# Expert rows left over from whole units: 22 tiles of 128 rows, or 8 tiles and 11 pairs of 64-row chunks

## The chip, the cores and the metric

The kernel runs on one core of one Trainium2 chip. The metric is the device time of one execution in microseconds. Three executions of the kernel before took 1140.57, 1143.54 and 1146.61 us (median 1143.54).

## The reference

One transformer layer on `x` of 4 x 1024 tokens of 256 float32 values: a Nystrom attention, then a mixture of 8 experts of which each token takes 2. Only the experts are touched by the change.

```python
x = x + attention(layernorm(x))        # 16 heads, 64 landmarks, pseudo-inverse, convolution of 13 taps
h_in = layernorm(x)                    # 4096 tokens of 256
logits = h_in @ router_w.T             # 8 experts
weights, selected = sparsemixer(logits) # two experts per token, one weight each
for e in range(8):
    h = silu(h_in @ w_gate[e].T) * (h_in @ w_up[e].T)      # 256 -> 512
    out += dense_w[:, e:e+1] * (h @ w_down[e].T)           # 512 -> 256
x = x + out
```

## The kernel before

The program is written out by hand, engine by engine, with semaphores; nothing reorders it. TensorE multiplies, ScalarE (`act`) applies functions and copies, VectorE (`dve`) does the elementwise work, GpSimd (`pool`) scatters rows by index, SyncE (`sp`) issues the plain transfers.

The router gives 8192 rows (4096 tokens, 2 experts each). GpSimd scatters each into the region of its expert in the scratch tensor `xs_d`; a row carries its 256 values, its weight and its token number. Then the rows are worked off in **items**. An item belongs to one expert and is a list entry in `ITEMS` with its number of 128-row blocks:

- 3 early items (5 blocks) of the fullest expert, while the router still works;
- 22 **units** of two blocks (`NU`), which are full but for the last rows of an expert;
- 22 **tiles** of one block (`NT`), for what is left of each expert. With 8 experts and ends that don't divide by 128 some rows of tiles are padding.

That is 71 blocks. VectorE works out which expert and which first row each unit and tile has, once the router's counts are there: `table` writes `u_eid`, `u_row` for units, and after `units_taken` the same for tiles.

Work goes in steps `n`, one step per block: a unit has two (its 512 inner columns in two halves), a tile one. In a step:

- TensorE `hidden(0, n)`: the gate product. Stationary is a 128x128 piece of the weights `wgu`, moving are the item's rows as columns (`xst`, 256 columns for a unit, 128 for a tile), two contractions of 128. The result has the inner dimension on partitions. Each float32 matmul stands in the trace as two passes.
- TensorE `x_columns(a+1)`: the next item's rows transposed into bank 7. `rows_transposed` on ScalarE copies them to `xst`.
- TensorE `down(n-1)`: stationary is the hidden block `hid` of the step before, moving are the down weights `w_d_s[:, e]` (256 columns), addressed by the expert's number in a register. Results go to bank 4 or 6.
- TensorE `hidden(1, n)`: the up product, like the gate.
- ScalarE `gate_out(n)`: the Silu of the gate. VectorE `hidden_out(n)`: times the up product, into `hid`.
- VectorE `rows_weighed(a-1)`: the down result times the row weights into one of 8 buffers `ys` (`YRING`). `expert_weights(a+2)` copies an expert's gate and up weights (128x2048) into one of two `wgu` buffers.
- GpSimd `add_rows`: an indirect transfer that adds the 128 rows to `out` by token number. Before an item's first store it waits until all stores of the item before have landed, since a token's two rows may lie in two items of different experts.
- SyncE `unit_rows`, `tile_rows`: an item's rows from `xs_d` into one of 16 slots `xs`.

The last item's stores end the kernel.

Of the kernel before, what the change touches and what calls it, by code (L numbers as in the profile page):

```python
# [27 lines left out]
P = 128  # L28
# [74 lines left out]
FIRST = NEARLY  # L103
CHOSEN = [i + 4 for i in DONE[:LATE]] + [QT + 1, QT + 2, QT + 4]
# [17 lines left out]
def down_bank(a, b):  # L122
    return 4 + 2 * (b if ITEMS[a] == 2 else a % 2)

# [43 lines left out]
def layer(nc, x, w_qkv, wq_t, wk_t, conv_band, w_fc, b_fc, router_t, w_gu, w_down, out):  # L168
    with ExitStack() as ctx:
# [112 lines left out]
        hid = ex[:, 0].rearrange("p (u c) -> p u c", u=2)  # L282

# [27 lines left out]
        assert NT <= NU  # L311
        t_tau, u_eid, u_row, t_eid, t_row = (sb(f"tab{i}", NU) for i in range(5))
        early = sb("early", 2)
        n_pad = sb("n_pad", E)
        tokid = sb("tokid", G * 2).rearrange("p (v c) -> p v c", v=G)
# [32 lines left out]
        def _(sp):  # L348
# [79 lines left out]
            def slot_free(a):  # L428
                for r in range(BLOCK[a] - XRING, BLOCK[a + 1] - XRING):
                    if r >= EBLK:  # L430
                        sp.wait_ge(s(f"m_sc{r % YRING}"), 16 * (r // YRING + 1))

            def unit_rows(i):
                a = FIRST + i
                v = (BLOCK[a] - EBLK) % XRING
                slot_free(a)
                r = sp.value_load(u_row[0:1, i:i + 1].bitcast(I32), min_val=0, max_val=ZROW - 2 * P)
                sp.dma_start(xs[:, v:v + 2], xs_d[bass.ds(r, 2 * P), :].rearrange("(u p) c -> p u c", p=P))\
                  .then_inc(s(f"m_rows_in{i % 8}"), 16)

            def tile_rows(i):
                a = FIRST + NU + i
                slot_free(a)
                sp.wait_ge(s("m_xtp"), a - 7)
                r = sp.value_load(t_row[0:1, i:i + 1].bitcast(I32), min_val=0, max_val=ZROW)
                sp.dma_start(xs[:, (BLOCK[a] - EBLK) % XRING], xs_d[bass.ds(r, P), :])\
                  .then_inc(s(f"m_rows_in{(NU + i) % 8}"), 16)

            for i in range(4):
                unit_rows(i)  # L450
            for e in range(E):
                pad_region(sp, e)
            for i in range(4, NU):
                unit_rows(i)
            sp.wait_ge(s("d_tiles"), 1)
# [1395 lines left out]
```

## Time and profile before

| | |
|---|---|
| median of the three executions | 1143.54 us |
| the profiled execution | 1153.58 us |
| its span | 1151.8 us |
| TensorE busy | 1100.0 us, 96% |
| VectorE, ScalarE, GpSimd busy | 632.0, 303.1, 300.5 us |
| mean granted clock of TensorE | 0.987 |
| units and tiles, from the first unit's gate product to the last down product | 783.4 to 1143.6 us |

The profile is one execution, a little slower than the three without profile. The span runs from the first to the last instruction. Busy shares are averages over stages; the stage of units and tiles is the last third. A row of the chain of waits is a piece of work that the next one waited for; in a timeline, the bracket behind a row is how long the engine was idle before it and what ended that.

### The profile page before, as it was taken

Reading aid. Unit: us, or ns where it says so; the run is one execution under the profiler, and the core shown is the slowest. Engines: PE = TensorE matmul, PEld = TensorE weight load, DVE = VectorE, ACT = ScalarE, POOL = GpSimd, SP = SyncE. Lnnn points to the kernel's source line nnn. Section 1 sums busy time; section 2 is a strip of 40 time slices with the busy share of each in tenths; the row PEclk is TensorE's granted clock in tenths of the full one; section 3 lists DMA queues with packets and bytes.
Section 4 is the critical chain, followed back from the end, with each engine's and each line's share of the span. In section 5 each row is a group of like instructions: output and inputs, shape, how many; then the busy total and the mean of one; then the engine's idle time right before and its main releaser. Section 6 shows DMA issues by size and latency. Waiting matters only on the chain.

```text
span 1151.8 us, 22825 instructions
## 1 busy us (share of the span) xinstructions
PE 1100.0 (96%) x9162; PEld 915.3 (79%) x9162; DVE 632.0 (55%) x1346; ACT 303.1 (26%) x457; POOL 300.5 (26%) x298
## 2 busy tenths in 40 slices
PE   4999999999989899999999999879999999999996
PEld 4887888888888656777776777767888888899996
DVE  7466666555478565586677677653233233234442
ACT  4433323332234421333233233221111111111110
POOL 6000000000200022244543563532322322334343
PEclk9999999999999999999999999889999999999998
DMA  9200000001200131222222233334323323221221
GB/s 340 107 1 1 1 1 1 1 1 38 57 3 1 52 134 37 102 74 86 101 83 75 76 103 122 111 87 101 48 49 52 47 49 52 34 46 35 45 27 11
DMA packets 48538, 68.91 MB, mean 60 GB/s; under 512 B 7872, under 2 KB 41792, under 8 KB 47424
## 3 DMA queue, kind: packets, MB, share of 16 engines
q1 hardware_dynamic: 34720, 47.50, 12.9%
q0 software_dynamic: 13296, 16.92, 8.8%
q10 hardware_dynamic: 432, 3.24, 0.7%
q8 instruction: 62, 1.02, 0.4%
q14 instruction: 28, 0.23, 0.1%
HBM read 42.10 MB, written 26.46 MB: 60 GB/s over the span
## 4 chain that ended last, share of the span: by engine, by line
PE 86%; DVE 7%; issue 2%; POOL 2%; ACT 1%; another core or an unknown queue 1%; POOLq 0%; DVEq 0%
PE ps L1737 20%; PE ps L1760 10%; PE ps L1624 10%; PE ps L1663 9%; PE ps L1375 9%; PE ps L1336 9%; PE ps L1655 5%; PE ps L1643 1%; PE ps L1490 1%; PE ps L1310 1%; PE ps L1720 1%; PE ps L1509 1%; ACT mem L691 1%; PE ps L1390 1%
## 5 line engine op out<-in xcount | busy, mean ns | idle before, releaser
L1737 PE MATMUL ps<-mem 128*128 128x256 f32 (+1 forms) x1504 | 259.9, 328 | 0.0
L1737 PEld LDWEIGHTS ps<-mem 128*128 128x128 f32 x1504 | 232.3, 191 | 21.2
L565 POOL DMA_INDIRECT out<-mem x71 | 122.9, 1731 | 255.8 <-DVE mem L1215 192.5
L1207 DVE TENSOR_TENSOR mem<-mem,ps 128x512 f32<-128x512 f32 x71 | 48.8, 687 | 171.6 <-PE ps L1737 143.1
L1760 PE MATMUL ps<-mem 128*128 x568 | 137.2, 385 | 5.1 <-DVE mem L1207 3.4
L535 POOL TENSOR_TENSOR mem<-mem,small 128x1024 f32<-128x1024 f32 x36 | 68.6, 1906 | 242.1 <-DVE small L1144 109.3
L1624 PE MATMUL ps<-mem 128*128 128x512 f32 x288 | 129.7, 594 | 1.3 <-DVE mem L1028 1.3
L771 ACT ACTIVATE mem<-ps 128x512 f32<-128x512 f32 x71 | 42.4, 597 | 320.9 <-PE ps L1737 314.7
L1760 PEld LDWEIGHTS ps<-mem 128*128 128x128 f32 x568 | 105.8, 193 | 18.4 <-issue 5.7
L1663 PE MATMUL ps<-mem 128*128 128x256 f32 x512 | 120.1, 388 | 0.0
L1375 PE MATMUL ps<-mem 128*128 128x256 f32 x512 | 119.2, 386 | 0.6 <-ACT mem L645 0.6
L1336 PE MATMUL ps<-mem 128*128 128x256 f32 x512 | 114.5, 380 | 0.0
L1663 PEld LDWEIGHTS ps<-mem 128*128 128x128 f32 x512 | 95.9, 192 | 14.1 <-issue 2.1
L1375 PEld LDWEIGHTS ps<-mem 128*128 128x128 f32 x512 | 95.9, 192 | 13.9 <-issue 0.8
L1336 PEld LDWEIGHTS ps<-mem 128*128 128x128 f32 x512 | 95.6, 190 | 12.7 <-issue 0.3
L1624 PEld LDWEIGHTS ps<-mem 128*128 128x128 f32 x288 | 54.2, 190 | 56.2 <-issue 52.7
L549 POOL DMA_INDIRECT xs_d<-mem,idx x64 | 62.5, 976 | 58.0 <-DVE idx L1124 37.9
L1655 PEld LDWEIGHTS ps<-mem 128*64 128x64 f32 x1152 | 58.0, 138 | 22.1 <-issue 22.1
L1215 DVE TENSOR_SCALAR mem<-ps,mem 128x256 f32<-128x256 f32 x71 | 32.1, 480 | 72.8 <-PE ps L1760 72.8
L1655 PE MATMUL ps<-mem 128*64 128x116 f32 x1152 | 66.1, 268 | 3.0 <-POOL mem L535 3.0
L746 ACT ACTIVATE mem<-ps 128x928 f32<-128x928 f32 (+2 forms) x36 | 31.5, 875 | 109.8 <-PE ps L1655 102.2
L1224 DVE COPY mem<-mem 128x2048 f32 x44 | 54.1, 1229 | 4.2 <-issue 0.9
(219 smaller groups left out, 1302.5 us busy)
## 6 DMA issues: line engine op xcount, KB each, us to landing
mem<-w_gu SPq DMA_DIRECT2D x9, 1024.0 KB, 5.1
mem<-xs_d SPq DMA_DIRECT2D x22, 260.0 KB, 2.8
mem<-x SPq DMA_DIRECT2D x8, 512.0 KB, 7.5
mem<-x SPq DMA_DIRECT2D x32, 128.0 KB, 2.2
out<-mem SPq DMA_DIRECT2D x32, 128.0 KB, 1.7
mem<-w_down SPq DMA_DIRECT2D x8, 512.0 KB, 5.8
xnt_d<-mem ACTq DMA_DIRECT2D x3, 1056.0 KB, 5.0
mem<-xnt_d SPq DMA_DIRECT2D x3, 1056.0 KB, 4.9
```

Of the source, the lines that this page charges most:

```text
L535: pool.tensor_tensor(a1[:, u], ex[:, u].rearrange("p (h c) -> p h c", h=H), ri[:, 16 * u:16 * u + 16].unsqueeze(2).to_broadcast([P, H, M]) ...
L549: pool.indirect_dma_start(out=xs_d, out_offset=bass.IndirectOffsetOnAxis(ap=idx[:, u, v, c:c + 1].bitcast(U32), axis=0), in_=xd[:, u, v, c ...
L565: pool.indirect_dma_start(out=out_rows, out_offset=bass.IndirectOffsetOnAxis(ap=rows[:, D + 1:D + 2].bitcast(U32), axis=0), in_=ys[:, r % ...
L1207: dve.tensor_tensor(hid[:, n % 2], sil[:, n % 2], bank(2 + n % 2), ALU.mult).then_inc(s("m_hid"), 1)
L1224: dve.tensor_copy(wgu[:, w % 2], w_gu_s[:, e]).then_inc(s("m_w"), 1)
L1336: mm = pe.matmul(bank(t // 2)[:, t % 2 * 2 * P:(t % 2 + 1) * 2 * P], xnts[b][:, k, HALO + P * t:HALO + P * t + P], g3c[:, b, k, j * P:(j + ...
L1375: mm = pe.matmul(bank(6)[:, k * 2 * P:(k + 1) * 2 * P], xna[:, b, t, k * P:(k + 1) * P], e3s[m % 4][:, t], start=(t == 0), stop=(t == RT - 1))
L1624: mm = pe.matmul(bank(2 * u + half), xnt2[b % 2][:, k, TO * t:TO * t + P], g1c[:, b, k, 512 * half:512 * half + 512], start=(k == 0), stop ...
L1655: mm = pe.matmul(bank(4, 2)[c:c + 64, (h // 2) * P:(h // 2) * P + TO], a1[:, q % 2, h], band[:, h], start=True, stop=True)
L1663: mm = pe.matmul(bank(6)[:, 0:D], cvt[:, j, at_:at_ + P], pm[:, b, j], start=(j == 0), stop=(j == J - 1))
L1737: mm = pe.matmul(bank(2 * c + n % 2)[:, i * size:(i + 1) * size], w[:, k, c, f * P:(f + 1) * P], xst[:, a % 2, k, 0:size], start=(k == 0), ...
L1760: mm = pe.matmul(bank(down_bank(a, b))[:, 0:D], hid[:, u, i * size + b * P:i * size + (b + 1) * P], w_d_s[:, e, f], start=(f == 0), stop=( ...
```

## The change

The padding of the tiles is cut by a smaller grain. Of an expert's rows, whole units are taken first, then whole tiles of 128 rows (8, `NT`), and what remains in **chunks** of 64 rows. Two chunks, mostly of two different experts, make a **pair** (11, `NP`): one block of 128 rows. The blocks are 68. Units and tiles keep their code; the order of items is 3 early, five rounds of 4 units and 2 pairs, 1 pair, 7 tiles, 2 units, 1 tile (`KIND`). A pair differs so:

- its two chunks come by two transfers, and the rows' token numbers are split in `half_to`, so that each of two stores writes one chunk; the second store waits for the landing of the first;
- hidden products: the rows are stationary, 64 columns a chunk, and the weights move, 512 columns; the first chunk works in columns 0 to 63 of the array, with its expert's weights taken by register from `w_gu_s`, the second in 64 to 127 with the copy in `wgu`. The result has rows on partitions;
- `inner_transposed`: `hid` is transposed in four pieces into bank 5, `inner_columns` on ScalarE copies them to `hidt`;
- `down`: stationary are 64 columns of `hidt` a chunk, moving the down weights of the first expert by register and of the second from `w_d_c`, a copy that `second_down_weights` on ScalarE makes; there is one such buffer. `down` of a pair stands behind `hidden(1)` of the next step, not ahead of it;
- VectorE makes one more table (`c_eid`, `c_row`, 22 chunks), in the second step of the first unit.

```diff
-NT = (LATER + E * (P - 1)) // P - 2 * NU
+NT = -(-(LATER - E * (P - 1)) // P) - 2 * NU
+C = P // 2
+NC = (LATER + E * (C - 1)) // C - 2 * (2 * NU + NT)
+NP = -(-NC // 2)
 EBLK = EROWS // P
-ITEMS = [2] * (EBLK // 2) + [1] * (EBLK % 2) + [2] * NU + [1] * NT
 NEARLY = EBLK // 2 + EBLK % 2
+ROUNDS = min(NU // 4, NP // 2)
+KIND = ["early"] * NEARLY + (["unit"] * 4 + ["pair"] * 2) * ROUNDS + ["pair"] * (NP - 2 * ROUNDS) + \
+       ["tile"] * (NT - 1) + ["unit"] * (NU - 4 * ROUNDS) + ["tile"]
+ITEMS = [2] * (EBLK // 2) + [1] * (EBLK % 2) + [2 if kind == "unit" else 1 for kind in KIND[NEARLY:]]
+ORDER = [KIND[:a].count(kind) for a, kind in enumerate(KIND)]
...
+def stores(r):
+
+    return sum(2 if KIND[STEP_OF[n][0]] == "pair" else 1 for n in range(r % YRING, r + 1, YRING))
+
+
+def loads(a):
+
+    return sum(2 if KIND[i] == "pair" else 1 for i in range(FIRST + (a - FIRST) % 8, a + 1, 8))
...
+        hidt = ex[:, 1, 0:F].rearrange("p (f c) -> p f c", f=4)
+        w_d_c = at(7 * SQ + 2 * G * 2 * ROW, 4 * D).rearrange("p (f c) -> p f c", f=4)
...
+            def item_rows(a):
+                i, v, landed = ORDER[a], (BLOCK[a] - EBLK) % XRING, s(f"m_rows_in{(a - FIRST) % 8}")
+                if KIND[a] == "unit":
+                    r = sp.value_load(u_row[0:1, i:i + 1].bitcast(I32), min_val=0, max_val=ZROW - 2 * P)
+                    sp.dma_start(xs[:, v:v + 2], xs_d[bass.ds(r, 2 * P), :].rearrange("(u p) c -> p u c", p=P)).then_inc(landed, 16)
+                if KIND[a] == "tile":
+                    if i == 0:
+                        sp.wait_ge(s("d_tiles"), 1)
+                    r = sp.value_load(t_row[0:1, i:i + 1].bitcast(I32), min_val=0, max_val=ZROW)
+                    sp.dma_start(xs[:, v], xs_d[bass.ds(r, P), :]).then_inc(landed, 16)
+                if KIND[a] == "pair":
+                    if i == 0:
+                        sp.wait_ge(s("d_chunks"), 1)
+                        sp.wait_ge(s("d_pad_out"), 16 * (E + 1))
+                    for q in range(2):
+                        r = sp.value_load(c_row[0:1, 2 * i + q:2 * i + q + 1].bitcast(I32), min_val=0, max_val=ZROW)
+                        sp.dma_start(xs[C * q:C * q + C, v], xs_d[bass.ds(r, C), :]).then_inc(landed, 16)
+
+            for a in range(FIRST, FIRST + 4):
+                item_rows(a)
...
+            ch.link(pool.memset(half_out[:, :], 2.0 * TOK))
+            for q in range(2):
+                ch.link(pool.affine_select(out=half_out[:, q:q + 1], in_=half_out[:, q:q + 1], compare_op=ALU.is_ge, fill=0.0,
+                                           base=(-C, C - 1)[q], pattern=[[0, 1]], channel_multiplier=(1, -1)[q]))
...
+                    rows = xs[:, (r - EBLK) % XRING]
+                    if KIND[a] == "pair":
+                        add_rows(r, half_to[:, ORDER[a] % 4, 0:1])
+                        wait_alone(pool, f"m_sc{r % YRING}", 16 * stores(r) - 16)
+                        add_rows(r, half_to[:, ORDER[a] % 4, 1:2])
+                    else:
+                        add_rows(r, rows[:, D + 1:D + 2])
 
...
+            def second_down_weights(a):
+                if ORDER[a] == 0:
+                    act.wait_ge(s("d_chunks"), 1)
+                e = act.value_load(c_eid[0:1, 2 * ORDER[a] + 1:2 * ORDER[a] + 2].bitcast(I32), min_val=0, max_val=E - 1)
+                if ORDER[a] >= 1:
+                    act.wait_ge(s("m_down"), BLOCK[max(b for b in range(a) if KIND[b] == "pair") + 1])
+                act.activation(w_d_c, w_d_s[:, e], ACT.Copy).then_inc(s("m_wdc"), 1)
+
+            def inner_columns(n):
+                a = STEP_OF[n][0]
+                act.wait_ge(s("m_ht"), ORDER[a] + 1)
+                if ORDER[a] >= 1:
+                    act.wait_ge(s("m_down"), BLOCK[max(b for b in range(a) if KIND[b] == "pair") + 1])
+                act.activation(hidt, bank(5).rearrange("p (f c) -> p f c", f=4), ACT.Copy).then_inc(s("m_hidt"), 1)
...
+                if KIND[STEP_OF[n - 1][0]] == "pair":
+                    inner_columns(n - 1)
+                if KIND[a] == "pair":
+                    second_down_weights(a)
                 if h == ITEMS[a] - 1 and a + 1 < len(ITEMS):
                     rows_transposed(a + 1)
...
+                    if KIND[a] == "pair":
+                        ch.link(dve.tensor_tensor(half_to[:, ORDER[a] % 4].bitcast(I32),
+                                                  rows[:, D + 1:D + 2].bitcast(I32).to_broadcast([P, 2]),
+                                                  half_out[:, :].bitcast(I32), ALU.add))
...
-            units_taken()
-            table(P, P - 1, 7, NT, t_eid, t_row, "d_tiles")
+            taken(NU, 2 * P)
+            table(P, 0, 7, NT, t_eid, t_row, "d_tiles")
             expert_weights(FIRST + 1)
             rows_weighed(1)
             hidden_out(4)
             dve.wait_ge(s("d_tiles"), 1)
             for n in range(BLOCK[FIRST], NSTEP):
                 a, h = STEP_OF[n]
-                if h == 0:
+                if h == 0 and KIND[a - 1] != "pair":
                     rows_weighed(a - 1)
                 hidden_out(n)
+                if h == 0 and KIND[a - 1] == "pair":
+                    rows_weighed(a - 1)
+                if n == BLOCK[FIRST] + 1:
+                    taken(NT, P)
+                    table(C, C - 1, 6, 2 * NP, c_eid, c_row, "d_chunks")
                 if h == ITEMS[a] - 1 and a + 2 < len(ITEMS):
                     expert_weights(a + 2)
...
+                if KIND[a] == "pair":
+                    if c == 0:
+                        if ORDER[a] == 0:
+                            pe.wait_ge(s("d_chunks"), 1)
+                        first_expert[a] = expert_of(c_eid, 2 * ORDER[a])
+                        pe.wait_ge(s("m_w"), a - FIRST + 1)
+                        pe.wait_ge(s("m_xst"), a + 1)
+                        pe.wait_ge(s("m_hid"), n - 1)
+                    for k in range(KD):
+                        for q in range(2):
+                            mm = pe.matmul(bank(2 * c + n % 2)[C * q:C * q + C], xst[:, a % 2, k, C * q:C * q + C],
+                                           (w_gu_s[:, first_expert[a]] if q == 0 else wgu[:, (a - FIRST) % 2])[:, k, c], start=(k == 0), stop=(k == KD - 1))
+                    mm.then_inc(s(("m_gate", "m_up")[c]), 1)
+                    return
...
+            def inner_transposed(n):
+                a = STEP_OF[n][0]
+                pe.wait_ge(s("m_hid"), n + 1)
+                if ORDER[a] >= 1:
+                    pe.wait_ge(s("m_hidt"), ORDER[a])
+                for f in range(4):
+                    mm = pe.transpose(bank(5)[:, f * P:(f + 1) * P], hid[:, n % 2, f * P:(f + 1) * P], idt)
+                mm.then_inc(s("m_ht"), 1)
 
             def down(n):
                 (a, h), u = STEP_OF[n], n % 2
-                e = expert(a)
-                pe.wait_ge(s("m_hid"), n + 1)
+                if KIND[a] != "pair":
+                    e = expert(a)
+                    pe.wait_ge(s("m_hid"), n + 1)
+                else:
+                    pe.wait_ge(s("m_hidt"), ORDER[a] + 1)
+                    pe.wait_ge(s("m_wdc"), ORDER[a] + 1)
                 size = ITEMS[a] * P
                 per = F // size
-                before = a - 2 if ITEMS[a] == 1 and ITEMS[a - 2] == 1 else a - 1
+                before = a - 2 if ITEMS[a] == 1 and a >= 2 and ITEMS[a - 1] == 1 else a - 1
                 if h == 0 and before >= 0:
                     pe.wait_ge(s("m_y"), BLOCK[before + 1])
-                for b in range(ITEMS[a]):
-                    for i in range(per):
-                        f = per * h + i
-                        mm = pe.matmul(bank(down_bank(a, b))[:, 0:D], hid[:, u, i * size + b * P:i * size + (b + 1) * P],
-                                       w_d_s[:, e, f], start=(f == 0), stop=(f == 3))
+                if KIND[a] == "pair":
+                    for f in range(4):
+                        for q in range(2):
+                            mm = pe.matmul(bank(down_bank(a, 0))[C * q:C * q + C, 0:D], hidt[:, f, C * q:C * q + C],
+                                           w_d_s[:, first_expert[a], f] if q == 0 else w_d_c[:, f], start=(f == 0), stop=(f == 3))
+                else:
...
                 hidden(0, n)
+                after_pair = KIND[STEP_OF[n - 1][0]] == "pair"
+                if after_pair:
+                    inner_transposed(n - 1)
                 if h == ITEMS[a] - 1 and a + 1 < len(ITEMS):
                     x_columns(a + 1)
-                if n > first:
+                if n > first and not after_pair:
                     down(n - 1)
                 hidden(1, n)
+                if after_pair:
+                    down(n - 1)
             down(NSTEP - 1)
```

On TensorE, a step of the tiles before (L1737 hidden products, L1720 `x_columns`, L1760 `down`):

```order
L1737 MATMUL ps<-mem 128x128 x8
L1737 MATMUL ps<-mem 128x128 [waits m_hid,m_xst,m_w]
L1737 MATMUL ps<-mem 128x128 x7
L1720 MATMUL ps<-ids,mem 128x128 [waits m_xst,m_rows_in3]
L1720 MATMUL ps<-ids,mem 128x128
L1746 TENSOR_LOAD tab
L1746 ISA x2
L1760 ISA [waits m_y,m_hid]
L1760 MATMUL ps<-mem 128x256
L1760 ISA
```

The second pair's step and the start of the unit behind it, in the changed program (L1804 hidden products of a pair, L1839 `inner_transposed`, L1784 `x_columns`, L1858 `down` of a pair, L1820 hidden products of a unit):

```order
L1804 ISA [waits m_hid,m_xst,m_w]
L1804 MATMUL ps<-mem 64x512 x2
...
L1839 MATMUL ps<-ids,mem 128x128 [waits m_hid]
L1839 MATMUL ps<-ids,mem 128x128 x3
L1784 MATMUL ps<-ids,mem 128x128 [waits m_xst,m_rows_in6]
...
L1804 MATMUL ps<-mem 64x512 x2
L1858 ISA [waits m_y,m_wdc,m_hidt]
L1858 MATMUL ps<-mem 64x256 x2
...
L1820 MATMUL ps<-mem 128x256 [waits m_hid,m_xst,m_w]
L1820 MATMUL ps<-mem 128x256 x3
```

The down products have moved from between the two hidden products of a step to behind both, directly ahead of the next item's gate product; the transposes of the inner rows are new.

On ScalarE, the tiles before (L771 `gate_out`, L764 `rows_transposed`):

```order
L771 ACTIVATE mem<-ps 128x512 [waits m_hid,m_gate]
L764 ACTIVATE mem<-ps 128x2x128 [waits m_up,m_xtp]
L771 ACTIVATE mem<-ps 128x512 [waits m_hid,m_gate]
L764 ACTIVATE mem<-ps 128x2x128 [waits m_up,m_xtp]
L771 ACTIVATE mem<-ps 128x512 [waits m_hid,m_gate]
```

And in the changed program, the second pair's step (L804 `gate_out`, L819 `inner_columns`, L809 and L812 `second_down_weights`, L797 `rows_transposed`):

```order
L804 ACTIVATE mem<-ps 128x512 [waits m_hid,m_gate]
L819 ACTIVATE mem<-ps 128x512 [waits m_down,m_ht]
L809 TENSOR_LOAD tab
L809 ISA x2
L812 ISA [waits m_down]
L812 ACTIVATE mem<-mem 128x1024
L797 ACTIVATE mem<-ps 128x512 [waits m_up,m_xtp]
L804 ACTIVATE mem<-ps 128x512 [waits m_hid,m_gate]
```

Between the gate's Silu and the copy of the next item's columns there are now the copy of the inner columns and the copy of the down weights, which waits for `m_down`.

## Rows read from the trace of the kernel before

**Rows 1.** The page, part 4: the chain that ended last, by engine
```profile
PE 86%; DVE 7%; issue 2%; POOL 2%; ACT 1%; another core or an unknown queue 1%; POOLq 0%; DVEq 0%
```

**Rows 2.** The chain in order of time, units: start us, us, what
```profile
990.81 3.45 PE ps L1737 x16
...
994.26 0.44 PE ps L1720 x4
...
1001.61 3.45 PE ps L1737 x16
```

**Rows 3.** The same view, tiles
```profile
1104.31 1.73 PE ps L1760 x8
...
1109.83 1.73 PE ps L1760 x8
```

**Rows 4.** The same view around one convolution (L1655)
```profile
654.09 1.74 PE ps L1655 x32
...
655.83 3.65 PE ps L1663 x16
...
659.48 3.43 PE ps L1624 x8
```

**Rows 5.** Groups by line and form, ScalarE: busy us, mean ns | idle before
```profile
L752 ACT ACTIVATE mem<-mem 128x1024 f32<-128x1024 f32 x36 | 37.9, 1052 | 18.5 <-DVE mem L1134 18.2
...
L764 ACT ACTIVATE mem<-ps 128x512 f32<-128x512 f32 x24 | 14.2, 592 | 8.3 <-PE ps L1720 8.3
...
L764 ACT ACTIVATE mem<-ps 128x256 f32<-128x256 f32 x23 | 8.7, 378 | 0.0
```

**Rows 6.** Timeline of the end: start us, us, engine, line, what
```profile
1138.97 0.49 DVE L1215 TENSOR_SCALAR mem<-ps,mem 128x256 f32<-128x256 f32 x1 [2.77 <-PE ps L1760]
...
1140.81 0.69 DVE L1207 TENSOR_TENSOR mem<-mem,ps 128x512 f32<-128x512 f32 x1 [1.35 <-PE ps L1737]
...
1141.65 1.99 PE L1760 MATMUL ps<-mem 128*128 x8 [0.94 <-DVE mem L1207]
...
1143.68 0.48 DVE L1215 TENSOR_SCALAR mem<-ps,mem 128x256 f32<-128x256 f32 x1 [2.18 <-PE ps L1760]
...
1145.32 1.56 POOL L565 DMA_INDIRECT out<-mem  x1 [3.46 <-issue]
```

**Rows 7.** Timeline, first unit: VectorE, and one TensorE row
```profile
772.76 0.17 DVE L1197 TENSOR_SCALAR small<-small 128x8 f32<-128x8 f32 x1
...
776.71 0.24 DVE L1192 TENSOR_SCALAR tab<-tab,small 128x22 int32<-128x22 f32 x1
...
777.46 1.23 DVE L1224 COPY mem<-mem 128x2048 f32 x1 [0.51 <-issue]
...
793.06 0.69 DVE L1207 TENSOR_TENSOR mem<-mem,ps 128x512 f32<-128x512 f32 x1 [4.93 <-PE ps L1737]
...
796.46 0.88 DVE L1215 TENSOR_SCALAR mem<-ps,mem 128x256 f32<-128x256 f32 x2 [1.41 <-PE ps L1760]
...
798.24 0.69 DVE L1207 TENSOR_TENSOR mem<-mem,ps 128x512 f32<-128x512 f32 x1 [0.91 <-issue]
...
800.15 1.89 PE L1760 MATMUL ps<-mem 128*128 x8
```

**Rows 8.** The chain in order of time, at the start
```profile
6.33 0.20 POOL validf L489
...
6.59 0.20 POOL validf L491
```

**Rows 9.** Timeline of GpSimd, last unit and first tile
```profile
1027.52 1.56 POOL L565 DMA_INDIRECT out<-mem  x1 [0.31 <-issue]
...
1032.98 1.55 POOL L565 DMA_INDIRECT out<-mem  x1 [3.89 <-issue]
```

**Rows 10.** Timeline of TensorE behind two waits
```profile
768.34 1.99 PE L1760 MATMUL ps<-mem 128*128 x8 [1.69 <-DVE mem L1215]
...
780.22 3.42 PE L1760 MATMUL ps<-mem 128*128 x8 [2.43 <-DVE mem L1207]
```

More of the change, by code:

```diff
@@ L103 @@
 FIRST = NEARLY
+assert all(ITEMS[a] == 1 or (BLOCK[a] - EBLK) % 2 == 0 for a in range(FIRST, len(ITEMS)))
 CHOSEN = [i + 4 for i in DONE[:LATE]] + [QT + 1, QT + 2, QT + 4]
@@ L441, in tile_rows @@
[L441 to L450, printed above, removed]
+                        sp.wait_ge(s(f"m_sc{r % YRING}"), 16 * stores(r))
@@ L451, in _ @@
+            for a in range(FIRST, FIRST + 4):
+                item_rows(a)
             for e in range(E):
                 pad_region(sp, e)
-            for i in range(4, NU):
-                unit_rows(i)
-            sp.wait_ge(s("d_tiles"), 1)
-            sp.wait_ge(s("d_pad_out"), 16 * (E + 1))
-            for i in range(NT):
-                tile_rows(i)
+            for a in range(FIRST + 4, len(ITEMS)):
+                item_rows(a)
             for v in range(YRING):
-                sp.wait_ge(s(f"m_sc{v}"), 16 * -(-(BLOCK[-1] - v) // YRING))
+                sp.wait_ge(s(f"m_sc{v}"), 16 * stores(max(r for r in range(BLOCK[-1]) if r % YRING == v)))
@@ L1031, in _ @@
                 ch.step(dve.tensor_copy(v, v.bitcast(I32)))
+            ch.step(dve.tensor_copy(half_out[:, :].bitcast(I32), half_out[:, :]))
             ch.sync()
@@ L1193, in table, with taken @@
                    .then_inc(s(done), 1)
[L1195 to L1197 removed]
+            def taken(count, rows):
+                ch.link(dve.tensor_scalar(te, te, -1.0, float(count), ALU.mult, ALU.add))
                 ch.link(dve.scalar_tensor_tensor(out=te, in0=te, scalar=0.0, in1=nt, op0=ALU.max, op1=ALU.min))
[L1199 to L1200 removed]
+                ch.step(dve.scalar_tensor_tensor(out=base, in0=te, scalar=float(rows), in1=base, op0=ALU.mult, op1=ALU.add))
+                ch.link(dve.scalar_tensor_tensor(out=n_e, in0=te, scalar=-float(rows), in1=n_e, op0=ALU.mult, op1=ALU.add))
             def hidden_out(n):
@@ L1218, in expert_weights @@
             def expert_weights(a):
-                w, n = a - FIRST, a - FIRST - NU
-                source = u_eid[0:1, w:w + 1] if n < 0 else t_eid[0:1, n:n + 1]
+                w, i = a - FIRST, ORDER[a]
+                source = {"unit": u_eid, "tile": t_eid, "pair": c_eid}[KIND[a]]
+                i = 2 * i + 1 if KIND[a] == "pair" else i
+                source = source[0:1, i:i + 1]
                 e = dve.value_load(source.bitcast(I32), min_val=0, max_val=E - 1)
@@ L1741, in expert @@
             def expert(a):
-                i, t = a - FIRST, a - FIRST - NU
-                if t == 0:
-                    pe.wait_ge(s("d_tiles"), 1)
-                source = early[0:1, 0:1] if i < 0 else u_eid[0:1, i:i + 1] if t < 0 else t_eid[0:1, t:t + 1]
-                return pe.value_load(source.bitcast(I32), min_val=0, max_val=E - 1)
+                if KIND[a] == "early":
+                    return expert_of(early, 0)
+                if KIND[a] == "unit":
+                    return expert_of(u_eid, ORDER[a])
@@ L1755, in down @@
                 if h == 0 and before >= 0:
                     pe.wait_ge(s("m_y"), BLOCK[before + 1])
-                for b in range(ITEMS[a]):
-                    for i in range(per):
-                        f = per * h + i
-                        mm = pe.matmul(bank(down_bank(a, b))[:, 0:D], hid[:, u, i * size + b * P:i * size + (b + 1) * P],
-                                       w_d_s[:, e, f], start=(f == 0), stop=(f == 3))
+                if KIND[a] == "pair":
[4 more added lines that the diff above has]
+                else:
+                    for b in range(ITEMS[a]):
+                        for i in range(per):
+                            f = per * h + i
+                            mm = pe.matmul(bank(down_bank(a, b))[:, 0:D], hid[:, u, i * size + b * P:i * size + (b + 1) * P],
+                                           w_d_s[:, e, f], start=(f == 0), stop=(f == 3))
```

39 lines of the change are left out of this document (18 added, 21 removed).

## The prediction, made before the changed kernel ran

> **What bounds the kernel now.** I read the page's chain of waits first: 86% of the span lies on TensorE [rows 1]. Then the same chain in order of time, over the stage that the change touches, because a share of the span says nothing about one stage. There TensorE's pieces follow each other without a hole: a unit (two blocks of 128 rows) has a period of 1001.61 - 990.81 = 10.80 us, 5.40 a block, with four transposes in 0.44, 0.109 each [rows 2]; a tile (one block) has 1109.83 - 1104.31 = 5.52 us [rows 3]. Nothing else is late in this stage, so a TensorE instruction taken out there is worth its time, and one put in, or a wait, costs its own.
>
> **What the change takes out.** Expert rows before: 5 early blocks, 22 units, 22 tiles, 71 blocks. After: 8 tiles and 11 pairs stand for the 22 tiles, 68 blocks. Fourteen tiles go: 14 x 5.52 = **-77.3 us** [rows 3].
>
> **What a pair costs on TensorE.** The hidden products of a pair are 8 matmuls of 512 columns with 64 stationary columns, each in the trace two passes: 16 passes, 8 in each column half. Eight passes of 512 columns take 3.43 us on the full array [rows 4], so 3.43 if the halves run side by side, 6.86 if not. The convolution is the one large user of column halves before: 32 passes of 116 columns in 1.74 us [rows 4]. At 3.43 / (8 x 512) us a column one after the other they would need 3.1, in two halves 1.55; the halves do overlap there. The down products are 16 passes of 256 columns, two halves: the 1.73 of a tile [rows 3]. New are four transposes of the inner rows, 0.44, and the two of the rows stay, 0.22. A pair: 3.43 + 1.73 + 0.44 + 0.22 = 5.82; eleven: **+64.0 us**. So a pair as such is 0.3 dearer than a tile, and three blocks fewer would leave -13.3.
>
> **Changes between full and half width.** The convolution takes 1.74 where its columns ask for 1.55, and the 16 passes of 256 columns after it take 3.65 [rows 4] where the same kind takes 2 x 1.73: 0.19 + 0.19 = 0.38 for going into halves and coming back. By the order, two pairs between units have four stretches of halves (first half of the hidden products of the first; its second half with the first of the next; the second half of that with down of the first; down of the last) and the three pairs in a row have five: 4 x 4 + 5 = 21. 21 x 0.38 = **+8.0 us**; bounds 21 x 0.19 = 4 and 21 x 0.5 = 10.
>
> **The wait that is added.** `second_down_weights(a)` copies the second expert's down weights on ScalarE (128x1024) into the one buffer `w_d_c`. For the second of two adjoining pairs it waits on `m_down` of the first. But TensorE now does that `down` last in the step, after `hidden(1, n)`, and behind the waiting copy in ScalarE's queue stands `rows_transposed(a+1)`, which TensorE's next instruction, `hidden(0, n+1)`, needs. So TensorE stands still for the whole way: end of matmul to the engine 0.04 and an address instruction 0.06 (an estimate), the copy 1.05 (the nearest row is the exponential of 128x1024 in memory, 1052 ns [rows 5]), the column copy 0.59 for a unit or 0.38 for a single block [rows 5], 0.10 of overlap between two ScalarE instructions (an estimate), 0.15 back to TensorE (1140.81 + 0.69 to 1141.65) [rows 6]: 1.79 or 1.58 us idle. An unstalled follower also overlaps the drain, 1.89 against 1.73, 0.16 [rows 3, 7], and 0.1 of the return from halves is hidden in the wait. Net 1.85 before a unit (four times), 1.74 before the third pair, 1.64 before a tile: **+10.8 us** for six. Bounds: the copy at half its time gives 7.6, a slower hand-over 13. A lone first pair has no such wait: its copy waits on a down that is long over and has `down` and `hidden(1)` of 3.4 us as cover. The inner-row copy to columns (`inner_columns`, 0.6) has the transposes and `hidden(1)`, 2.2 us, as cover and costs nothing; without that cover it would cost 0.6 a pair.
>
> **The chunk table on VectorE.** `taken` and `table` run once more, in the first unit's second step. The same work took from 772.76 to 776.95, 4.2 us, and 0.5 passed until the copy behind it began [rows 7]. Placed after the 0.69 that starts at 793.06, it ends near 797.9; the weight copy (1.23) then runs to 799.7, `rows_weighed` (0.88) to 800.5, and the product that began at 798.24 begins 2.2 later. Before, the product was there at 799.1 with its 0.15 of hand-over and TensorE asked at 800.15 [rows 7]; now it is there at 801.3: **+1.1 us** (0 to 2.2).
>
> **Start and end.** Three short GpSimd instructions are added ahead of `consts`. GpSimd's constants are on the chain from the first microsecond, 0.26 from one such instruction to the next [rows 8]: **+0.7 us** (0.5 to 0.8). At the end the last tile now follows a unit, not a tile. A unit's second store starts 1.56 + 0.31 = 1.87 behind its first; the start after it came 1032.98 - 1027.52 = 5.46 later [rows 9], as it waits for the landing. In the last step the tile's rows come 4.7 behind the unit's (the two VectorE starts at 1138.97 and 1143.68 are as far apart), and their store would start 1.15 after them (1143.68 + 0.48 to 1145.32 [rows 6]), at 5.85; through the unit's stores it starts at 1.15 + 1.87 + 5.46 = 8.5. That is 2.6; I take **+2.2 us** because landings are uneven, bounds 0 and 2.6.
>
> **Nothing for:** GpSimd's two stores per pair, one after the other's landing, some 10.9 us a pair against 8 on TensorE. Eight buffers (`YRING`) lie between, and each unit gives back 10.8 - 7.3 = 3.5. The seven tiles behind the three pairs hold the lag of about 8 us near constant; that is below two blocks. Nothing for SyncE: `item_rows` of the first pair stands behind `d_chunks` (near 798) and is needed four units on, near 821.
>
> **Sum.** -77.3 + 64.0 + 8.0 + 10.8 + 1.1 + 0.7 + 2.2 = **+9.5 us**. The profiled execution took 1153.58, so 1163.1 there; the median of the runs shown is 1143.54, and nothing in the sum depends on the 10 us between them: 1153.0.
>
> **Rivals.**
> 1. *TensorE's clock falls in the new waits.* After 1.69 us idle eight passes still took 1.99; after 2.43 us idle the same took 3.42, half speed, which is the lower level of 1.2 GHz [rows 10]. The new waits of 1.6 to 1.8 lie near the first and short of the second. Each fall costs about 3.42 - 1.73 = 1.7. Two to six falls: +3.4 to +10.2, 1156 to 1163. Chance 0.2.
> 2. *The halves overlap only in part.* For: two 512-column streams side by side are longer than any before. Against: [rows 4]. The other end of the bound is 3.43 + 1.73 = 5.16 more a pair, 11 times: 1210. Overlap wanting a quarter: about +15, 1168. Chance 0.06. The Trainium skill, "TensorE: Matmul & The Clock Gate", Measured speedup vs the span model, gives 2.38 times for three column tiles, 0.79 of the ideal; an estimate by that page is 5.16 / 0.79 - 5.16 = 1.4 more a pair, 1168 in all. This case's trace does not agree so far: 3.1 / 1.74 is 1.8 times of a possible 2, with the change of width included.
> 3. *Not slower: the copy hardly holds TensorE.* If ScalarE's copy in memory is much quicker than the exponential, or the way through the two semaphores shorter, the six waits shrink. At 0.9 us each the sum is +3.9, 1147; with no wait at all it is -1.3, 1142. From under 1.2 us a wait on the case is inside half a per cent. For it: no row shows a plain copy of this shape. Against: two of the three rows of the chain are measured, and the order leaves no other work between [rows 5, 6]. Chance 0.24. Only if the changes of width were free as well would the kernel be faster: -13.3 + 1.1 + 0.7 + 2.2 = -9.3, 1134; that is 0.05 of these 0.24.
>
> **Numbers.** Likeliest is the sum, chance 0.5, own range 1149 to 1158 from the bounds of the waits and of the width changes. The range for 8 in 10 takes in most of rival 1 and the better half of rival 3: 1145 to 1164. A measurement of this kernel tells about half a per cent (5.7 us; the three runs shown spread over 6.0) from no change. Slower by more: 0.75 (the forecast, rivals 1 and 2, less a little); within: 0.20; faster by more: 0.05.
>
> **What would show it.** In the changed profile: passes of 512 columns with 64 stationary columns in couples, about 1.7 us for each half of the hidden products (above 2.0 speaks for rival 2); six idle pieces of TensorE of 1.6 to 1.8 us with ScalarE's column copy as what ended them, and the weight copy before it near 1.05 us; a granted clock that stays at 1.00 behind them (rival 1 if not); two single tiles still at 5.52; one piece of about 1 us near 800 us; the last store starting about 8 us, not 6, after the weighing of the rows before it. I am wrong if the idle pieces are missing, or if TensorE's time for two pairs without them is far from 2 x 5.82 + 4 x 0.38 = 13.2 us.

## The result, and the profile after

| | before | changed |
|---|---|---|
| median (range, runs) | 1143.53 us (1140.57 to 1146.61, 4) | 1152.74 us (1151.76 to 1154.46, 4) |
| profiled execution, its span | 1153.58, 1151.8 | 1151.76, 1149.9 |
| matmul passes of TensorE, its busy time | 9162, 1100.0 us | 8992, 1088.0 us |

The changed kernel is slower: ratio 1.0078, 95% interval [1.006, 1.0096], 9.2 us on the medians. The two profiled executions stand the other way round: that of before took 1153.58 us, while the 51 other executions of it on record took 1140.6 to 1147.2. The chain of waits of before, in order of time (start us, us, what):

```profile
744.44 6.25 another core or an unknown queue
...
750.74 3.63 another core or an unknown queue
```

The view's chain of the changed kernel begins only at 789.64 us, so it can't tell of this place; ScalarE's timeline can. Ahead of the Silu at 750.71 and the activation at 754.38 ScalarE idled 6.28 and 3.07 us before, and no such piece (0 and 0.89 us) ahead of the same two at 741.00 and 742.46 in the changed kernel. So the two are compared by stages that begin after it, or end before it.

**The waits behind the second pair.** The chain of the changed kernel in order of time, second pair of the first round (L1804 hidden products of a pair, L1839 `inner_transposed`, L1784 `x_columns`, L1858 `down` of a pair, L1820 hidden products at full width), with the five later idle pieces:

```profile
824.45 1.87 PE ps L1804 x8
826.32 1.73 PE ps L1858 x16
828.04 1.79 issue
829.83 1.96 PE ps L1820 x8
...
886.00 1.79 issue
...
943.97 1.79 issue
...
1001.92 1.79 issue
...
1059.66 1.68 issue
...
1067.67 1.57 issue
```

Six pieces, 10.41 us together, where [rows 2, 3] have none. "Issue" says that the view found no releaser. The timeline of the same microseconds shows one (start us, us, engine, line, tile and shape, in brackets the idle time before and what ended it):

```profile
826.15 1.90 PE L1858 MATMUL ps<-mem 128*64 x16
...
828.19 1.06 ACT L812 ACTIVATE mem<-mem 128x1024 f32 x1 [3.54 <-PE ps L1858]
...
829.15 0.58 ACT L797 ACTIVATE mem<-ps 128x512 f32<-128x512 f32 x1
...
829.83 0.89 PE L1820 MATMUL ps<-mem 128*128 128x256 f32 x3 [1.79 <-issue]
```

ScalarE idles 3.54 us until TensorE's `down` ends, copies the weights in 1.06, then the columns in 0.58, and 0.10 after those TensorE starts.

**The stages.** At the table of chunks, the chain:

```profile
790.03 0.61 DVE mem L1260
790.64 0.14 issue
790.78 1.99 PE ps L1864 x8
792.77 3.45 PE ps L1820 x16
```

This `down` at 790.78 is the one that stands at 800.15 before [rows 7]. The end, timeline:

```profile
1134.05 0.88 DVE L1272 TENSOR_SCALAR mem<-ps,mem 128x256 f32<-128x256 f32 x2 [2.77 <-PE ps L1864]
1135.48 1.56 POOL L592 DMA_INDIRECT out<-mem  x1 [7.33 <-DVE mem L1272]
...
1136.73 1.99 PE L1864 MATMUL ps<-mem 128*128 x8 [0.94 <-DVE mem L1260]
1137.35 1.56 POOL L592 DMA_INDIRECT out<-mem  x1 [0.30 <-issue]
1138.76 0.48 DVE L1272 TENSOR_SCALAR mem<-ps,mem 128x256 f32<-128x256 f32 x1 [2.18 <-PE ps L1864]
1142.03 1.56 POOL L592 DMA_INDIRECT out<-mem  x1 [3.13 <-DMA out<-mem]
```

And TensorE's first instruction, timeline of before and of the changed kernel:

```profile
14.81 0.79 PE L1297 MATMUL ps<-ids,mem 128*128 128x136 f32 x2 [14.81 <-DVE mem L832]
```

```profile
15.44 0.79 PE L1361 MATMUL ps<-ids,mem 128*128 128x136 f32 x2 [15.44 <-DVE mem L884]
```

| stage | before | changed | difference | the prediction's terms |
|---|---|---|---|---|
| start to TensorE's first | 14.81 | 15.44 | +0.63 | +0.7 |
| `down` at the table to the last `down` | 800.15 to 1141.65 = 341.50 | 790.78 to 1136.73 = 345.95 | +4.45 | -77.3 + 64.0 + 8.0 + 10.8 = +5.5 |
| wait at the table | none | see the run e7_all | +1.0 | +1.1 |
| last `down` to the end of the span | 10.15 | 13.17 | +3.0 | +2.2 |

Together 9.1, and the medians are 9.2 apart. Between the first and the second stage nothing is changed but the wait at the table. The profiled execution of before took 11.0 us more there (14.81 to 800.15, against 15.44 to 790.78 less the wait); the two pieces of its chain shown above are 9.9 of them. That the other executions of both kernels take equal times there is taken for granted, not measured.

**A rule for reading the experiments.** Executions of one kernel differ by the mean clock that was granted to TensorE: before took 1141.1 us at a mean of 0.996 and 1147.2 at 0.990. One slope (0.86 us for 0.001) and a level for each kernel, fitted to the 109 executions whose clock is on record, leave 0.7 us of scatter. At a mean clock of 0.992 the levels are: before 1144.8, changed 1153.4, e1_rows_first 1142.2, e2_two_buffers 1142.2, e6_halves_in_turn 1153.1, e7_all 1140.4, e8_one_run 1137.7, e9_tiles_between 1140.3, e10_down_in_turn 1163.6. Where medians are close I read these beside the ratios.

### The profile page after: what moved, and what is told of

The parts are those of the page before. It is cut to its first block and busy times, and to the rows that moved or that the text cites. A ratio compares the mean times of both kernels' runs of the same rounds, so it can differ in the third digit from the quotient of the medians.

```text
span 1149.9 us, 22649 instructions
## 1 busy us (share of the span) xinstructions
PE 1088.0 (95%) x8992; PEld 864.5 (75%) x8992; DVE 631.2 (55%) x1369; ACT 318.5 (28%) x473; POOL 309.3 (27%) x309
## 5 line engine op out<-in xcount | busy, mean ns | idle before, releaser
L1820 PE MATMUL ps<-mem 128*128 128x256 f32 (+1 forms) x1056 | 210.0, 352 | 8.7 <-issue 8.7
L1820 PEld LDWEIGHTS ps<-mem 128*128 128x128 f32 x1056 | 179.0, 191 | 32.6 <-issue 12.8
L592 POOL DMA_INDIRECT out<-mem x57 | 94.0, 1650 | 187.9 <-DVE mem L1272 145.4
L804 ACT ACTIVATE mem<-ps 128x512 f32<-128x512 f32 x68 | 40.6, 597 | 285.6 <-PE ps L1820 241.7
L1864 PE MATMUL ps<-mem 128*128 x456 | 111.5, 389 | 6.5 <-DVE mem L1260 4.2
L1400 PEld LDWEIGHTS ps<-mem 128*128 128x128 f32 x512 | 95.6, 190 | 12.7 <-issue 0.3
L1727 PEld LDWEIGHTS ps<-mem 128*128 128x128 f32 x512 | 94.7, 190 | 13.7 <-issue 2.1
L1439 PEld LDWEIGHTS ps<-mem 128*128 128x128 f32 x512 | 94.7, 190 | 13.4 <-issue 0.8
L1864 PEld LDWEIGHTS ps<-mem 128*128 128x128 f32 x456 | 85.4, 194 | 17.8 <-issue 7.4
L1688 PEld LDWEIGHTS ps<-mem 128*128 128x128 f32 x288 | 54.2, 190 | 56.2 <-issue 52.7
L592 POOL DMA_INDIRECT out<-mem,half_to x22 | 37.5, 1703 | 68.0 <-DMA out<-mem,half_to 43.1
```

Of the source, the lines that this page charges most:

```text
L592: pool.indirect_dma_start(out=out_rows, out_offset=bass.IndirectOffsetOnAxis(ap=rows_to.bitcast(U32), axis=0), in_=ys[:, r % YRING], in_of ...
L1400: mm = pe.matmul(bank(t // 2)[:, t % 2 * 2 * P:(t % 2 + 1) * 2 * P], xnts[b][:, k, HALO + P * t:HALO + P * t + P], g3c[:, b, k, j * P:(j + ...
L1439: mm = pe.matmul(bank(6)[:, k * 2 * P:(k + 1) * 2 * P], xna[:, b, t, k * P:(k + 1) * P], e3s[m % 4][:, t], start=(t == 0), stop=(t == RT - 1))
L1688: mm = pe.matmul(bank(2 * u + half), xnt2[b % 2][:, k, TO * t:TO * t + P], g1c[:, b, k, 512 * half:512 * half + 512], start=(k == 0), stop ...
L1727: mm = pe.matmul(bank(6)[:, 0:D], cvt[:, j, at_:at_ + P], pm[:, b, j], start=(j == 0), stop=(j == J - 1))
L1820: mm = pe.matmul(bank(2 * c + n % 2)[:, i * size:(i + 1) * size], w[:, k, c, f * P:(f + 1) * P], xst[:, a % 2, k, 0:size], start=(k == 0), ...
```

## Experiments

### The copy behind the columns (e1_rows_first)

The columns of the next item are copied ahead of the weights, so TensorE's next product no longer stands behind the copy that waits.

```diff
-                if KIND[a] == "pair":
-                    second_down_weights(a)
                 if h == ITEMS[a] - 1 and a + 1 < len(ITEMS):
                     rows_transposed(a + 1)
+                if KIND[a] == "pair":
+                    second_down_weights(a)
```

> In ScalarE's queue rows_transposed(a+1) stands ahead of second_down_weights(a); all else is the changed kernel's. Theory (the next item's columns wait behind the weight copy, which waits for the down product): the six idle pieces of TensorE of 1.57 to 1.79 us are gone, net -10.8 us against the changed kernel, some 1142 us, about the time of the kernel before. Rival (the wait only moves, since one buffer w_d_c still has to be refilled between two adjoining pairs): down of the second pair waits on m_wdc, six idle pieces of about 1 us in another place, 1148 or more.

Measured: 1142.14 us (10 runs), ratio to before 0.9982 [0.9968, 0.9997]. Against the changed kernel that is 1.0% or 11 us. Timeline of the same place:

```profile
826.52 1.90 PE L1858 MATMUL ps<-mem 128*64 x16
...
828.35 1.99 PE L1820 MATMUL ps<-mem 128*128 128x256 f32 x8
...
828.57 1.06 ACT L812 ACTIVATE mem<-mem 128x1024 f32 x1 [3.06 <-PE ps L1858]
```

The copy still waits for `down`, still takes 1.06, and now nobody waits for it. From the `down` at the table (791.15) to the last one (1126.28) there are 335.13 us against 345.95: 10.8 less, which is the term of the sum. The rival, six waits in another place, fell.

### Two buffers for the copy (e2_two_buffers)

The order of ScalarE's work is that of the changed kernel; the copy waits for the `down` of the pair before last.

```diff
-        w_d_c = at(7 * SQ + 2 * G * 2 * ROW, 4 * D).rearrange("p (f c) -> p f c", f=4)
+        w_d_c = at(7 * SQ + 2 * G * 2 * ROW, 8 * D).rearrange("p (u f c) -> p u f c", u=2, f=4)
...
-                if ORDER[a] >= 1:
-                    act.wait_ge(s("m_down"), BLOCK[max(b for b in range(a) if KIND[b] == "pair") + 1])
-                act.activation(w_d_c, w_d_s[:, e], ACT.Copy).then_inc(s("m_wdc"), 1)
+                if ORDER[a] >= 2:
+                    act.wait_ge(s("m_down"), BLOCK[[b for b in range(a) if KIND[b] == "pair"][-2] + 1])
+                act.activation(w_d_c[:, ORDER[a] % 2], w_d_s[:, e], ACT.Copy).then_inc(s("m_wdc"), 1)
...
```

> Two buffers for the second chunk's down weights, so that the copy waits for the down product of the last pair but one; ScalarE's order stays. Theory: that wait alone held the queue, so it is over early and the six idle pieces are gone here too, about 1142 us, equal to the run with the order changed within 0.3%. Rival (it is the length of ScalarE's queue, 0.6 + 0.6 + 1.05 + 0.6 us in one step, not the wait): rows_transposed ends late still, some 0.3 to 1 us idle at each of the six places, 1145 to 1148.

Measured: 1142.99 us (10 runs), ratio 0.9978 [0.9957, 0.9999]. Timeline:

```profile
827.19 1.06 ACT L812 ACTIVATE mem<-mem 128x1024 f32 x1
828.15 0.58 ACT L797 ACTIVATE mem<-ps 128x512 f32<-128x512 f32 x1
...
828.62 1.90 PE L1858 MATMUL ps<-mem 128*64 x16
```

The copy is done before `down` begins, the columns 0.1 us after it has begun, and the idle pieces are gone. So it was the copy's wait for the one buffer together with its place, not the 1.06 us of work added to ScalarE: taking away either is enough, and both give the same time.

### The hidden products half after half (e6_halves_in_turn)

```diff
-                    for k in range(KD):
-                        for q in range(2):
+                    for q in range(2):
+                        for k in range(KD):
```

> The hidden products of a pair with the half as the outer loop: two matmuls of the first half, then two of the second, instead of alternating. Theory A (overlap needs neighbours in different halves, as the convolution's order 0,1,1,0 gives them in couples): the 16 passes of 512 columns take about 6.9 us a pair instead of 3.5, +3.4 x 11 = +38 us, about 1190. Theory B (each half has its own queue and starts when it is free): no change, 1153. Strict order with overlap only at the border would give about +28, 1181.

Measured: 1153.59 us (4 runs), ratio 1.0084 [1.0059, 1.011], that of the changed kernel. Starts of the passes of 512 columns with 64 stationary columns in one half of a hidden product, in ns, from the trace (first half of the array / second half): 817183 / 817197, 817663 / 817677, 818093 / 818106, 818522 / 818535. In the changed kernel, where the halves alternate in the program: 815808 / 815814, 816288 / 816294, 816717 / 816724, 817146 / 817153. Though four passes of the first half stand ahead of it in the program, the first pass of the second half starts 14 ns after the first of them. The halves overlap in full either way, and the time is that of theory B. The Trainium skill ("TensorE: Matmul & The Clock Gate", The mechanism) says that matmuls start and end strictly in the program's order; between column halves this trace does not agree.

### Both products of a pair half after half (e10_down_in_turn)

The same exchange of loops in the down products as well, where one half has eight passes.

```diff
-                    for f in range(4):
-                        for q in range(2):
+                    for q in range(2):
+                        for f in range(4):
```

> The changed kernel with both products of a pair written half after half: hidden as in run e6_halves_in_turn, and the down product with its 8 passes of the first half before the 8 of the second. Theory (each column half has its own queue, and the second half's passes start as soon as they are handed over, whatever stands between them in the program): no change, 1153, the down product of a pair still about 1.7 to 1.9 us. Rival (only a few passes ahead can be taken past a busy half; the hidden product has 4 passes of a half in a row, the down product 8): part of each down product is done one half after the other, up to 1.7 us more for each of 11 pairs, so 1160 to 1172.

Measured: 1163.66 us (4 runs), ratio 1.0169 [1.0147, 1.0191], so 0.9% or 10 us above the changed kernel. The theory fell and the rival came true. The chain:

```profile
825.06 2.63 PE ps L1858 x16
827.70 1.78 issue
```

The down product takes 2.63 for 1.73: 0.90 more, 9.9 for eleven pairs. Its passes start at 824887, 825102, 825318, 825534, 825750 ns in the first half, and the second half's first at 825756: it gets its first pass when the first half begins its fifth of eight, and so in all eleven pairs. Four passes of 216 ns are 0.86 us. As far as these two lengths show, the second half starts early only while no more than four passes of the first stand ahead of it; with four, as in the run before this one, nothing is lost. What sets the four was not tried.

### All repairs at once, and three tiles at the end (e7_all)

The edit of e1_rows_first; the table in the first unit's first step; the three GpSimd constants behind the start's own; and the tiles last:

```diff
-       ["tile"] * (NT - 1) + ["unit"] * (NU - 4 * ROUNDS) + ["tile"]
+       ["tile"] * (NT - 3) + ["unit"] * (NU - 4 * ROUNDS) + ["tile"] * 3
...
-                if n == BLOCK[FIRST] + 1:
+                if n == BLOCK[FIRST]:
                     taken(NT, P)
                     table(C, C - 1, 6, 2 * NP, c_eid, c_row, "d_chunks")
```

> The changed kernel with four edits: rows_transposed ahead of second_down_weights; the chunk table in the first unit's first step, where VectorE has 4.9 us idle; three tiles instead of one behind the last two units; the constants for half_to built after the row statistics. Theory: 1152.7 - 10.8 (waits) - 1.1 (table) - 2.2 to -3 (last store) - 0.6 (start) = 1137 to 1138.5, so below both kernels. Rival (the waits are worth less, since what follows is late anyway): 1143 to 1148.

Measured: 1141.03 us (12 runs), ratio 0.9971 [0.9957, 0.9986]. I had expected about 3 us less. Two of the repairs do what they should. TensorE, timeline of e1_rows_first and then of this kernel:

```profile
791.15 1.99 PE L1864 MATMUL ps<-mem 128*128 x8 [0.82 <-DVE mem L1260]
```

```profile
14.75 0.79 PE L1361 MATMUL ps<-ids,mem 128*128 128x136 f32 x2 [14.75 <-DVE mem L884]
...
792.21 0.60 PE L1784 MATMUL ps<-ids,mem 128*128 128x128 f32 x4
792.65 1.68 PE L1864 MATMUL ps<-mem 128*128 x7
```

The start is back at 14.75, and the wait at the table is gone. The end is not shorter. The chain there runs over GpSimd's stores alone, and no longer over TensorE:

```profile
1093.64 5.24 DMA out<-mem
...
1105.08 3.74 DMA out<-mem
...
1124.34 3.80 DMA out<-mem
...
1129.01 3.70 DMA out<-mem
```

From the start of TensorE's last single pass to the end of the trace it takes 12.1 us, in e1_rows_first 11.5 (the table of stages counts from the first of the same eight passes, 1.6 us earlier). Each store waits for the landing of the one before, 4.6 to 4.7 us from start to start (1124.34, 1129.01, 1133.59), and with three pairs and five tiles shortly ahead GpSimd is still behind when the last tiles come. Three tiles at the end shorten it only if the queue of stores is empty by then.

### The same with tiles ahead of later rounds (e9_tiles_between)

```diff
-KIND = ["early"] * NEARLY + (["unit"] * 4 + ["pair"] * 2) * ROUNDS + ["pair"] * (NP - 2 * ROUNDS) + \
-       ["tile"] * (NT - 1) + ["unit"] * (NU - 4 * ROUNDS) + ["tile"]
+TURN = ["unit"] * 4 + ["pair"] * 2
+KIND = ["early"] * NEARLY + TURN * 2 + ["pair"] * (NP - 2 * ROUNDS) + ["tile"] * (NT - 3) + TURN * (ROUNDS - 2) + \
+       ["unit"] * (NU - 4 * ROUNDS) + ["tile"] * 3
```

> The kernel of run e7_all with its order changed alone: five of its tiles stand ahead of the later rounds of units and pairs, and three tiles close the list, so that GpSimd has units before the last tiles in which to catch up. Theory (the end of e7_all was late since GpSimd's stores, 4.65 us each, had not caught up with the pairs and tiles in one run): the last store starts soon after its rows are ready, from TensorE's last down product to the end 9.4 to 10 us instead of 12.05, time 1138 to 1139. Rival (the end is long for another reason): no change from e7_all, 1141.

Measured: 1141.62 us (11 runs), ratio 0.9972 [0.9958, 0.9986], no different from e7_all. In the profiled execution the end is 10.7 us for 12.1, so the queue of stores was part of it. But 0.7 to 1.3 us of what I expected is missing (9.4 to 10), and neither medians nor levels show the 1.4. The last stores are still a chain of landings, timeline:

```profile
1114.66 1.56 POOL L593 DMA_INDIRECT out<-mem  x1 [0.30 <-issue]
1119.16 1.56 POOL L593 DMA_INDIRECT out<-mem  x1 [2.94 <-DMA out<-mem]
1123.85 1.55 POOL L593 DMA_INDIRECT out<-mem  x1 [3.13 <-DMA out<-mem]
1128.37 1.56 POOL L593 DMA_INDIRECT out<-mem  x1 [2.96 <-DMA out<-mem]
```

The second store of a unit leaves a lag, and a tile gives back only 5.52 - 4.6 = 0.9 us of it; two tiles before the last don't clear it. Why the executions without a profile show nothing of the 1.4 stays open: the intervals of the two ratios don't exclude it, but the fitted levels (0.1 apart, with a 95% interval of 0.6) do. So whether the shorter end is worth anything is not shown.

### Eleven pairs in one run (e8_one_run)

The repairs of e7_all, one tile at the end, and:

```diff
-KIND = ["early"] * NEARLY + (["unit"] * 4 + ["pair"] * 2) * ROUNDS + ["pair"] * (NP - 2 * ROUNDS) + \
-       ["tile"] * (NT - 1) + ["unit"] * (NU - 4 * ROUNDS) + ["tile"]
+KIND = ["early"] * NEARLY + ["unit"] * 4 + ["pair"] * NP + ["tile"] * (NT - 1) + ["unit"] * (NU - 4) + ["tile"]
...
-        half_to = sb("half_to", 8).rearrange("p (u q) -> p u q", u=4)
+        half_to = sb("half_to", 16).rearrange("p (u q) -> p u q", u=8)
...
```

> The changed kernel with the rows' transposition ahead of the weights' copy, the table of pairs and the start's constants early, and another order: after the first 4 units all 11 pairs in one run, then 7 tiles, the other units, and one tile at the end. Changes between full width and halves fall from 21 to 13. Theory (0.38 us each on TensorE, everything else hidden): rows first alone gave 1142.1, less 0.7 for the start and 8 x 0.38 = 3.0 for the changes (some of the 0.8 at the table too): 1137.5, range 1136 to 1139. Rival: GpSimd's two dependent stores per pair (about 9.2 us against TensorE's 5.8 per pair) fall behind over 11 pairs by some 29 to 37 us, more than the buffers ahead of them hold, and TensorE is held in the run of pairs: 1141 or more, with idle TensorE in it that VectorE's wait for a buffer explains.

Measured: 1137.11 us (7 runs), ratio 0.9939 [0.9918, 0.996]: as expected, and the best of all. The chain inside the run of pairs repeats with 6.12 us:

```profile
824.67 1.73 PE ps L1857 x16
826.40 1.72 PE ps L1803 x8
828.12 0.59 PE ps L1838 x4
828.71 0.22 PE ps L1783 x2
828.93 1.87 PE ps L1803 x8
830.79 1.73 PE ps L1857 x16
```

No piece is idle. The sum says 5.82 + 0.38 for one change of width a pair = 6.20. What the change of width costs can be read here: the second half of a hidden product takes 1.87 for 1.72, the four transposes behind column halves 0.59 for 0.44, 0.30 together. From the `down` behind the table (792.81 in the chain of e7_all, 789.62 in that of this kernel) to the start of the last pass (1129.29 and 1123.29) the 8 changes fewer give 336.5 - 333.7 = 2.8 us, 0.35 each. GpSimd falls behind as the rival said (stores of pairs 4.64 us apart, 828.08 to 925.57 for 22 of them, so 9.3 a pair against 6.12 on TensorE), but the eight buffers hold, and the tiles and units behind give it back:

```profile
1109.80 1.56 POOL L591 DMA_INDIRECT out<-mem  x1 [7.38 <-DVE mem L1271]
```

## Why the prediction was right

- **Fourteen tiles less, eleven pairs more, changes of width.** In the chain of the changed kernel one round of four units and two pairs takes 886.00 - 828.04 = 57.96 us with its wait. Less the wait of 1.79 and 4 x 10.80 for the units, two pairs cost 12.97; the prediction had 13.2 for them. The halves overlap in full, which only the convolution [rows 4] had spoken for. The 0.38 a change is 0.30 by the rows of e8_one_run and 0.35 by its difference to e7_all. That the stage came out at +4.45 for +5.5 is this small excess, some 0.1 a pair, over eleven pairs. This 1.05 too much and the 0.8 too little at the end nearly cancel: that the sum lies within 0.3 us of the measured 9.2 is in part luck.
- **The wait behind the copy.** Predicted 1.79 or 1.58 idle, measured 1.79, 1.79, 1.79, 1.79, 1.68, 1.57; predicted +10.8 in all, measured 10.8 by taking it away. The exponential's row (1052 ns [rows 5]) was a good stand-in for a copy of the same shape (1.06). One piece is off: before the third pair 1.58 idle was forecast, as before any single block, and it has 1.68.
- **The table:** +1.1 predicted, 0.98 measured (the `down` of two blocks earlier starts at 779.00, so 5.40 a block would give 789.80, and it is 790.78). **Start:** +0.63 for +0.7, and e7_all gets it back.
- **The end** was mis-sized: +3.0 for +2.2, over the bound of 2.6. The order of stores is as predicted, and worth less: the last store starts 5.30 us behind the last `down` (1136.73 to 1142.03), before 3.67 [rows 6], so +1.6 for +2.2. I had left out what follows it: from its start to the end of the span 7.9 us pass, before 6.5, another +1.4. The transfers show where most of it comes from. The last store of before (1145.32), then of the changed kernel (1142.03): the GpSimd queue's packets and MB, and us from issue to landing

```profile
q0 software_dynamic: 144, 0.00, 1.1%
out<-mem POOLq DMA_INDIRECT x1, 2.7
```

```profile
q0 software_dynamic: 144, 0.13, 15.1%
out<-mem POOLq DMA_INDIRECT x1, 3.8
```

Before, the last two tiles held no row of any expert, only padding: in their stores the 128 packets for the rows have 8 bytes each, and the last one landed in 2.7. The changed kernel's last tile is full, 128 packets of 1 KB, and lands in 3.8. That is 1.1 of the 1.4, and the sum had priced the last store of both kernels alike.
- **Rival 1, the clock in the waits:** did not happen. The first eight passes behind a wait before a unit take 1.96 or 1.97, where half speed would be 3.42 [rows 10], and the windows of the stage give:

```profile
800.00:1100.00 300.00, 289.60 (x1557) 223.75 (x1556) 102.39 (x148) 61.26 (x108) 104.70 (x64) 1.00 0.28 42
```

(us, busy time of TensorE, its weight loads, VectorE, ScalarE and GpSimd, then the granted clock, 1.00: the upper level, 2.4 GHz). Waits of 1.79 us here stayed without a fall; 2.43 had one [rows 10].
- **Rival 2, halves that overlap in part:** fell with the couples of passes, 6 to 8 ns apart in a couple and 429 ns from couple to couple, and with 1.72 for half of a hidden product. Two halves gain the full factor of 2. The Trainium skill's figure for three column tiles ("TensorE: Matmul & The Clock Gate", Measured speedup vs the span model) is 2.38 times, 0.79 of the ideal; the two halves of this trace lose no such share.
- **Rival 3, the copy hardly holds TensorE:** fell; e1_rows_first is what the kernel is without the wait, and it lies 2 to 3 us under before. That is the -1.3 of the rival's own sum, and a little more for the excess of the pairs.
- **Costs set at nothing:** right in the changed kernel, GpSimd's stores and SyncE hold nobody up in the middle; a pair's two stores took 9.3 us (e8_one_run) where 10.9 was reckoned with. They are not free for good: e7_all shows GpSimd's lag at the end as soon as the order gives it no time.

## What to carry to other kernels

A finer grain took out tiles worth 77 us and put pairs worth 64 in their place; what it could gain were the 13 us between, and changes of width, waits, table, start and end cost more than that. The part that decided the sign was one copy of 1.06 us that waited for a buffer with the next product's operand queued behind it: its six waits cost 10.8 us, and without them the kernel is 2 to 3 us under before. So before adding a wait to an engine, list what stands behind it in that queue. Here each change between full width and column halves and back cost 0.30 to 0.35 us, so items of one kind belong in one run as long as the slowest queue beside them (here GpSimd's stores, 9.3 us a pair) has buffers to fall behind into and work afterwards to catch up. When two executions that were profiled contradict the medians, compare by stages.

## What the hardware showed beyond expectation

- The two column halves of TensorE take their passes apart from each other, out of the program's order: the second half's first pass started 14 ns after the first half's with four passes of the first ahead of it in the program, and 0.87 us after with eight ahead, when the fifth had begun.
- Two 512-column streams side by side with weights from two places run at 429 ns a pass each, no slower than one on the full array (3.43 us for eight [rows 4]).
- GpSimd's accumulating stores that wait for each other's landing take about 4.6 us from start to start (1119.16 to 1123.85 in e9_tiles_between, 4.64 on average over 22 half stores in e8_one_run). A chunk's store is hardly cheaper than a tile's, because it still hands over 128 packets, those of rows that it doesn't write with 8 bytes: with 64 rows written 4.59 (834.09 to 838.68 in the changed kernel), with none 3.60 (1074.23 to 1077.83). So on that queue a finer grain pays for the count of stores, and a store of nothing but padding still costs most of a full one.
- Six waits of TensorE of 1.57 to 1.79 us left the granted clock at 1.00 in the changed kernel.
